# Two graph layers on one core: the plain fields of each step's edges are copied by ScalarE instead of GpSimd

## The chip, the cores and the metric

The kernel runs on one core of a Trainium2 chip. A core has five engines that run their own instruction streams and meet at semaphores: TensorE (PE in the profile, its weight loads PEld), VectorE (DVE), ScalarE (ACT), GpSimd (POOL) and SyncE (SP), which here only issues DMAs. The metric is the device time of one execution in microseconds (us); the median of three runs before the change is 1748.61 us (1748.29 to 1752.34).

## The reference

2500 nodes with 1024 features, 80000 edges sorted by destination, two layers:

```python
h = relu(layernorm(x));  x = x + segment_sum((h @ W0)[src] * edge_w[:, None], dst)
h = relu(layernorm(x));  # second layer: edges plus self loops, row = src, col = dst
hh = h @ W1.T + b;  deg = count(row);  norm = deg[row]**-0.5 * deg[col]**-0.5
x = x + segment_sum(norm[:, None] * hh[col], row)
```

## The kernel before

The sparse sums are done as dense products. The 2500 nodes are 20 tiles of 128 rows. For each tile of destinations the kernel builds the 128 x 2560 matrix of edge weights (stored as A, in two half-precision parts) and the matrix of edge counts (C), multiplies A by the support h @ W0 (first layer), and later C by the scaled h (second layer).

**How A and C are built.** A *window* is 4 destination rows; four windows are a *quad*, eight quads (q0 to q7) make a tile; there are 160 quads. A *step* takes 8 *touches*, blocks of 128 edges in a table `etab` in SBUF (four fields for each edge: a key, and the three "plain" fields: column, weight, rest of the weight). For a step of quad n:

- **fields** (GpSimd, L516 to L527): for each window a register load gives the block number (L522), a cast copies the three plain fields to `fbuf` (L525) and an addition writes the key (L527). Two slots of `fbuf`: the fields of a step wait until the one-hots of the step two before are done (`hots_ready`).
- **one_hots** (VectorE, L764 to L776): four operations (L769, L771, L774, L775) turn `fbuf` into the operands of the step's matmuls. They wait for the fields (`step_fields`) and for TensorE to have used the slot (`step_used`).
- **step** (TensorE, L1265): eight matmuls into a PSUM pair.
- **window_out** (ScalarE, L1048 to L1050): when the step is used, three copies from PSUM to a staging slot in SBUF; two staging slots, so it also waits for the DMA stores of the quad two before (`st_out`).
- **second_part** (VectorE, L820 and L823) and **sum_counts** (GpSimd, L540, the degrees) follow window_out; then SyncE stores the quad to DRAM (L346, L348).
- After a tile's last quad SyncE transposes the tile of A back from DRAM (L357), before it issues the stores of the next quads: its queue is in order.

The order is written out by hand. The quads 0 to 15 run among the support products. From quad 16 on a quad's step stands beside 15 matmuls of the dense product of an earlier tile (L1316), which is what fills TensorE. The quads 0 to 31 have 4 touches in a window, so two steps each; the other 128 have 2 touches and one step. VectorE's order in a quad n is one_hots(n), second_part(n - 1), then `further`, a register load and a branch (more edges, if a window has them); q1 has a residual in it as well (L838), q2 the moments (L848). GpSimd's order is fields of quad n + 1, then sum_counts(n - 1). The last 128 quads are in loops: VectorE and TensorE go round once for two tiles (16 quads), ScalarE once for one tile, GpSimd once for two quads. From 1090 us on the second layer runs, which the change doesn't touch.

Of the kernel before, what the change touches and what calls it, by code (L numbers as in the profile page):

```python
# [6 lines left out]
def gnn_two_layers(nc, x, src, dst, edge_weight, w0, w1, b1, out):  # L7
    f32, i32, f16 = mybir.dt.float32, mybir.dt.int32, mybir.dt.float16
    ALU = mybir.AluOpType
    ACT = mybir.ActivationFunctionType  # L10
    AX = mybir.AxisListType

    P = 128
    N, D = x.shape
    E = src.shape[0]
    T = -(-N // P)
    LAST = N - (T - 1) * P
    NCH = E // P
# [6 lines left out]
    QPT = WPT // 4  # L25
    NW = WPT * T
    NQ = NW // 4
    NB = NW // P
    UP, UL = 4, 2
    PRE = 2  # L30
    PQ = PRE * QPT
    UQ = 4 * QPT
# [7 lines left out]
    F = 4  # L40
# [20 lines left out]
    with ctx:  # L61
        def sb(name, shape, dt):
            return ctx.enter_context(nc.sbuf_tensor(name, shape, dt))

        def sem(name):
            return ctx.enter_context(nc.semaphore(name))
# [6 lines left out]
        fbuf = sb("fbuf", [P, FS + 1, F, 8, 2], f16)  # L73
# [7 lines left out]
        negbase = sb("negbase", [P, NW], f32)  # L81
# [73 lines left out]
        def hot(s):  # L155


            return slots[:, s * SS:(s + 1) * SS].rearrange("p (t c) -> p t c", c=CS)
# [3 lines left out]
        def twice(a, shape):  # L162

            return a.unsqueeze(len(shape) - 1).to_broadcast(shape)
# [5 lines left out]
        etab_c = etab[:, 0:CP * F].rearrange("p (c f) -> p c f", f=F)  # L170
# [18 lines left out]
        wtab = area[0:1, ROW:ROW + 4 * NW].bitcast(i32)  # L189
# [17 lines left out]
        etab_ready = sem("etab_ready")  # L207
# [15 lines left out]
        sup_hi = sem("sup_hi")  # L223
        sup_ready = sem("sup_ready")
        sup_free = sem("sup_free")
        step_fields = sem("step_fields")
        hots_plain = sem("hots_plain")
        hots_ready = sem("hots_ready")
# [53 lines left out]
        def win_pair(e, pre=False):  # L282

            return WIN if e == 0 or pre else TP

        def need(eng, s, value):

            if not isinstance(value, int) or value > 0:
                eng.wait_ge(s, value)
# [192 lines left out]
        def _(pool):  # L482
# [34 lines left out]
            def fields(n, s, v0, count, u):  # L517


                need(pool, hots_ready, n - 1)  # L520
                for w in range(count):
                    pool.load(regs, wtab[0:1, bass.ds((v0 + w) * 4, 1)])  # L522
                    c = pool.snap(regs[0], min_val=0, max_val=NCH)
                    at = slice(w * u, (w + 1) * u)
                    pool.tensor_copy(fbuf[:, s, 1:F, at].rearrange("p f u d -> p u f d"),  # L525
                                     twice(etab_c[:, bass.ds(c, u), 1:F], [P, u, F - 1, 2])).then_inc(step_fields, 1)
                    pool.tensor_tensor(fbuf[:, s, 0, at], twice(etab_c[:, bass.ds(c, u), 0], [P, u, 2]),  # L527
                                       twice(negbase[:, bass.ds(v0 + w, 1)], [P, u, 2]), ALU.add).then_inc(step_fields, 1)

            def step_pre(n):  # L530
                fields(n, n % 2, 2 * n, 2, UP)
# [12 lines left out]
            for t in range(STEP0, T):  # L544
# [10 lines left out]
                w = t - STEP0  # L555
# [21 lines left out]
        def _(dve):  # L577
# [178 lines left out]
            def columns(touches, n):  # L756
                return iota_r[:, 0:n].rearrange("p (n d) -> p n d", d=2).unsqueeze(1).to_broadcast([P, touches, n // 2, 2])

            def part(touches, a, n):
                return touches[:, :, a:a + n].rearrange("p t (n d) -> p t n d", d=2)  # L760
# [2 lines left out]

            def one_hots(n, s):  # L764

                dve.wait_ge(step_fields, 2 * UP_STEPS(n))

                need(dve, step_used, n - 1)
                nc.vector.tensor_tensor(part(hot(s), M0, SB), columns(8, SB), by_touch(s, 1, 8, SB),  # L769
                                        ALU.is_equal).then_inc(hots_plain, 1)  # L770
                nc.vector.tensor_tensor(part(hot(s), 0, P), columns(8, P), by_touch(s, 0, 8, P), ALU.is_equal)  # L771

                dve.wait_ge(hots_plain, n + 1)
                nc.vector.tensor_tensor(part(hot(s), W0C, SB), part(hot(s), M0, SB), by_touch(s, 2, 8, SB), ALU.mult)  # L774
                nc.vector.tensor_tensor(part(hot(s), W1C, SB), part(hot(s), M0, SB), by_touch(s, 3, 8, SB),  # L775
                                        ALU.mult).then_inc(hots_ready, 1)  # L776

            def UP_STEPS(n):

                return 2 * n + 2 if isinstance(n, int) and n < 2 * UQ else 4 * n - 4 * UQ + 4  # L780
# [246 lines left out]
        def _(act):  # L1027
# [9 lines left out]
            def window_out(n, s, steps_done, pre=False):  # L1037

                act.load(regs, wtab[0:1, bass.ds(n * 16 + 15, 1)])
                through = act.snap(regs[0], min_val=1, max_val=MOST + 1)  # L1040
                pair = win_pair(s, pre)
                sums = pair[:].rearrange("p (w x) -> p w x", w=4)

                need(act, st_out[s], STORED(n, s))
                need(act, win_sum, n - 1)
                act.wait_ge(step_used, steps_done)
                act.wait_ge(further_used, through)
                act.activation(c_stage(s), sums[:, :, 0:SB], ACT.Copy)  # L1048
                act.activation(a_stage(s)[:, 0], sums[:, :, SB:2 * SB], ACT.Copy, scale=A_DOWN)
                act.activation(a_stage(s)[:, 2], sums[:, :, 2 * SB:3 * SB], ACT.Copy, scale=A_DOWN).then_inc(win_act, 1)  # L1050

            def STORED(n, s):

                return 48 * (n // 2) if isinstance(n, int) else 24 * n - 24 * s

            def tile(td):
                for q in range(QPT):
                    n = QPT * (td + PRE) + q
                    window_out(n, q % 2, 2 * n + 2 if isinstance(n, int) and n < UQ else n + UQ + 1)

            def split_block(g):
# [8 lines left out]
            def std(g):  # L1070
                t0, n = X_GROUPS[g]
                act.wait_ge(var_ready, g + 1)
                act.activation(scale[:, t0:t0 + n], scale[:, t0:t0 + n], ACT.Sqrt).then_inc(std_ready, 1)
# [37 lines left out]
            for t in range(T):  # L1111
                if t > 0:
                    sup_first(t - 1)
                if t + 1 < T:
                    transposed(t + 1)
                if t + 2 < T:
                    rows_normal(t + 2)
                if t == 0:
                    std(2)
                if t == STEP0 - 1:  # L1120
                    act.wait_ge(table_ready, 1)
                if t == min(W1_AT):
                    act.wait_ge(w_pow, 2)
                for g in W1_AT.get(t, ()):
                    split_block(g)
                w = t - STEP0
                if 0 <= w < PQ:
                    if w in (1, 6, 9):
                        std({1: 3, 6: 4, 9: 5}[w])
                    window_out(w, w % 2, 2 * w + 2, True)  # L1130
            sup_first(T - 1)

            for td in range(UQ // QPT - PRE):
                tile(td)
            with act.Fori(UQ // QPT - PRE, T - PRE) as td:
                tile(td)

            def counts_first(e, done):
                act.wait_ge(self_ready[e], done)
# [330 lines left out]
```

## Time and profile before

| | |
|---|---|
| median of three runs | 1748.61 us |
| the profiled execution: its own time | 1750.08 us |
| its span, first to last instruction | 1748.3 us |
| granted TensorE clock, mean | 0.966 |
| busy: PE, DVE, ACT, POOL | 89%, 53%, 26%, 32% of the span |
| stretches: support and quads 0 to 15 / quads 16 to 31 / the loops | up to 392 / 398 to 513 / 513 to 1090 us |

A row of the timeline gives an instruction's start and duration in us, engine, line, operation, what it writes and reads, and in brackets the idle time of its engine before it with the one that released it. The engines with a q (POOLq, ACTq) are the sequencers that load registers and hand instructions to their engine.

### The profile page before, as it was taken

How to read it: one execution, taken by the hardware profiler on the slowest of the kernel's cores; microseconds unless marked ns; L12 is line 12 of the kernel's file. 1: busy time of each engine (PE TensorE's matmuls, PEld its weight loads, DVE VectorE, ACT ScalarE, POOL GpSimd, SP SyncE). 2: the span in 40 equal slices, each digit the busy share in tenths (PEclk: the TensorE clock that was granted, in tenths of full speed). 3: DMA queues.
4: the chain of work that ended last, by engine and by line, in shares of the span. 5: the costliest groups of instructions: out<-in, count | busy, mean ns of one | idle time of the engine just before them, and what ended most of it. 6: DMA issues, size and time to landing. Idle time of an engine off the chain costs nothing.

```text
span 1748.3 us, 30157 instructions
## 1 busy us (share of the span) xinstructions
PE 1554.0 (89%) x8627; PEld 792.7 (45%) x8628; DVE 930.2 (53%) x1747; ACT 456.5 (26%) x783; POOL 556.2 (32%) x1494
## 2 busy tenths in 40 slices
PE   2566699995979999999998999979999999999998
PEld 1233355543545454444554545334444444444443
DVE  6956556425977678777776776382313131313121
ACT  2514454531212222222222222271212121212110
POOL 0112444213656677677676774000000000000000
PEclk9977899997989999999999999999999999999999
DMA  7201242107546565666565666671232323232310
GB/s 262 97 1 32 64 139 61 29 16 165 114 97 141 125 142 135 144 145 139 133 151 129 146 140 150 201 230 55 63 99 66 96 66 96 66 96 66 96 37 25
DMA packets 449659, 185.86 MB, mean 106 GB/s; under 512 B 376677, under 2 KB 431993, under 8 KB 449544
## 3 DMA queue, kind: packets, MB, share of 16 engines
q1 hardware_dynamic: 449544, 184.63, 41.5%
q8 instruction: 34, 0.56, 0.1%
q14 instruction: 81, 0.66, 0.1%
HBM read 77.06 MB, written 77.11 MB: 88 GB/s over the span
## 4 chain that ended last, share of the span: by engine, by line
PE 54%; DVE 14%; issue 11%; POOLq 5%; POOL 5%; DMA 4%; SPq 4%; DVEq 2%; ACT 2%; ACTq 0%
PE pair L1392 19%; PE pair L1304 12%; PE pair L1253 9%; PE pair L1316 7%; PE pair L1265 5%; POOLq L522 3%; POOL fbuf L525 2%; SPq L357 2%; POOL fbuf L527 2%; DVE slots L774 2%; DMA a_scratch<-area 2%; DVE slots L775 2%; DVE h L939 1%; PE pair L1422 1%; SPq L378 1%
## 5 line engine op out<-in xcount | busy, mean ns | idle before, releaser
L1316 PE MATMUL pair<-h,area 128*128 128x512 f16 x2400 | 551.0, 383 | 2.6 <-issue 1.9
L1316 PEld LDWEIGHTS pair<-h,area 128*128 128x128 f16 x2400 | 234.2, 99 | 265.5 <-issue 18.2
L1265 PE MATMUL pair<-slots 128*128 128x240 f16 x1624 | 209.3, 275 | 104.8 <-DVE slots L775 54.6
L525 POOL CAST fbuf<-etab 128x12 f16 (+1 forms) x640 | 192.9, 301 | 152.4 <-DVE slots L775 79.2
L1048 ACT ACTIVATE area<-pair 128x320 f32<-128x320 f32 x160 | 69.9, 437 | 643.2 <-PE pair L1265 439.9
L1265 PEld LDWEIGHTS pair<-slots 128*128 128x128 f16 x1624 | 157.3, 100 | 171.4 <-issue 73.0
L979 DVE SCALAR_TENSOR_TENSOR agg_s<-pair,sc,agg_s 128x512 f16<-128x512 f32 x40 | 28.2, 747 | 350.7 <-ACT agg_s L1172 350.7
L1304 PE MATMUL pair<-wmat,agg_t 128*128 128x512 f16 x960 | 210.4, 379 | 1.6 <-ACT agg_t L1179 1.6
L527 POOL TENSOR_TENSOR fbuf<-etab,negbase 128x4 f16 (+2 forms) x640 | 200.9, 314 | 0.0
L1392 PE MATMUL pair<-h,etab 128*128 128x512 f16 x800 | 182.1, 379 | 8.9 <-DVE h L939 8.7
L1392 PE MATMUL pair<-h,slots 128*128 128x512 f16 x800 | 180.5, 379 | 0.0
L540 POOL TENSOR_TENSOR deg_acc<-deg_acc,area 128x320 f32<-128x320 f32 x160 | 144.0, 900 | 109.1 <-ACT area L1050 108.8
L769 DVE TENSOR_TENSOR slots<-iota_r,fbuf 128x640 f16<-128x640 f16 x192 | 99.3, 517 | 136.0 <-POOL fbuf L527 52.3
L1304 PEld LDWEIGHTS pair<-wmat,agg_t 128*128 128x128 f16 x960 | 92.3, 98 | 112.7 <-ACT agg_t L1179 1.8
L1253 PE MATMUL pair<-wmat,agg_t 128*128 128x512 f16 x480 | 114.7, 399 | 21.4 <-issue 21.4
L771 DVE TENSOR_TENSOR slots<-iota_r,fbuf 128x1024 f16<-128x1024 f16 x192 | 132.7, 691 | 0.0
L820 DVE SCALAR_TENSOR_TENSOR area<-pair,area 128x320 f16<-128x320 f32 x160 | 77.5, 484 | 93.4 <-ACT area L1050 93.2
L1253 PE MATMUL pair<-wmat,xt 128*128 128x512 f16 x480 | 108.8, 384 | 0.0
L1172 ACT ACTIVATE agg_s<-pair,sc 128x512 f16<-128x512 f32 x40 | 25.3, 683 | 314.1 <-PE pair L1394 314.1
L1392 PEld LDWEIGHTS pair<-h,etab 128*128 128x128 f16 x800 | 63.6, 97 | 82.0 <-DVE h L939 12.4
L774 DVE TENSOR_TENSOR slots<-slots,fbuf 128x640 f16<-128x640 f16 x192 | 98.6, 513 | 0.0
L775 DVE TENSOR_TENSOR slots<-slots,fbuf 128x640 f16<-128x640 f16 x192 | 98.5, 513 | 0.0
(181 smaller groups left out, 1316.1 us busy)
## 6 DMA issues: line engine op xcount, KB each, us to landing
c_scratch<-area SPq DMA_DIRECT2D x160, 160.0 KB, 2.2
a_scratch<-area SPq DMA_DIRECT2D x320, 80.0 KB, 2.2
area<-c_scratch SPq DMA_DIRECT2D x20, 1280.0 KB, 7.3
xt<-in_x SPq DMA_DIRECT2D x19, 512.0 KB, 3.6
x_scratch<-xt SPq DMA_DIRECT2D x19, 512.0 KB, 2.9
xt<-x_scratch SPq DMA_DIRECT2D x19, 512.0 KB, 3.6
out_x<-xt SPq DMA_DIRECT2D x19, 512.0 KB, 2.6
h<-x_scratch SPq DMA_DIRECT2D x4, 2048.0 KB, 10.5
```

Source lines behind the costliest of these rows:

```text
L525: pool.tensor_copy(fbuf[:, s, 1:F, at].rearrange("p f u d -> p u f d"), twice(etab_c[:, bass.ds(c, u), 1:F], [P, u, F - 1, 2])).then_inc(s ...
L527: pool.tensor_tensor(fbuf[:, s, 0, at], twice(etab_c[:, bass.ds(c, u), 0], [P, u, 2]), twice(negbase[:, bass.ds(v0 + w, 1)], [P, u, 2]), A ...
L540: pool.tensor_tensor(deg_acc[:], deg_acc[:], c_stage(s), ALU.add).then_inc(win_sum, 1)
L769: nc.vector.tensor_tensor(part(hot(s), M0, SB), columns(8, SB), by_touch(s, 1, 8, SB), ALU.is_equal).then_inc(hots_plain, 1)
L771: nc.vector.tensor_tensor(part(hot(s), 0, P), columns(8, P), by_touch(s, 0, 8, P), ALU.is_equal)
L774: nc.vector.tensor_tensor(part(hot(s), W0C, SB), part(hot(s), M0, SB), by_touch(s, 2, 8, SB), ALU.mult)
L775: nc.vector.tensor_tensor(part(hot(s), W1C, SB), part(hot(s), M0, SB), by_touch(s, 3, 8, SB), ALU.mult).then_inc(hots_ready, 1)
L1253: last = pe.matmul(dest[:, half * H:(half + 1) * H], h_t(t)[:, q, k, :], wmat[:, r, k, half * H:(half + 1) * H], start=k == q == r == 0, s ...
L1265: return pe.matmul(dest, touches[:, t, 0:P], touches[:, t, P:CS], start=first, stop=last, skip_group_check=True)
L1304: return pe.matmul(WO[:, half * H:(half + 1) * H], agg_t[:, q, k, :], wmat[:, r, k, half * H:(half + 1) * H], start=k == q == r == 0, stop ...
L1316: last = pe.matmul(sum_pair(e)[:, half * H:(half + 1) * H], wts(e)[:, q, k, :], hpart(k, r)[:, half * H:(half + 1) * H], start=k == q == r ...
L1392: pe.matmul(AGG[:, half * H:(half + 1) * H], lhs, h_of(q)[:, half * H:(half + 1) * H], start=first and q == 0, stop=last and q == 1, skip_ ...
```

## The change

ScalarE gets a function `fields` of its own, which loads the block number for each window and copies the three plain fields with an ACTIVATE; GpSimd keeps the key (L527) and the degrees (L540). There are two semaphores, `step_keys` and `step_fields`, and one_hots waits for both. ScalarE's copies for quad n + 2 stand directly ahead of window_out(n). ScalarE's loop is one iteration shorter, with the last tile written out behind it.

```diff
--- before.py
+++ after.py
@@ -223,6 +223,7 @@
         sup_hi = sem("sup_hi")
         sup_ready = sem("sup_ready")
         sup_free = sem("sup_free")
+        step_keys = sem("step_keys")
         step_fields = sem("step_fields")
         hots_plain = sem("hots_plain")
         hots_ready = sem("hots_ready")
@@ -522,10 +523,8 @@
                     pool.load(regs, wtab[0:1, bass.ds((v0 + w) * 4, 1)])
                     c = pool.snap(regs[0], min_val=0, max_val=NCH)
                     at = slice(w * u, (w + 1) * u)
-                    pool.tensor_copy(fbuf[:, s, 1:F, at].rearrange("p f u d -> p u f d"),
-                                     twice(etab_c[:, bass.ds(c, u), 1:F], [P, u, F - 1, 2])).then_inc(step_fields, 1)
                     pool.tensor_tensor(fbuf[:, s, 0, at], twice(etab_c[:, bass.ds(c, u), 0], [P, u, 2]),
-                                       twice(negbase[:, bass.ds(v0 + w, 1)], [P, u, 2]), ALU.add).then_inc(step_fields, 1)
+                                       twice(negbase[:, bass.ds(v0 + w, 1)], [P, u, 2]), ALU.add).then_inc(step_keys, 1)
 
             def step_pre(n):
                 fields(n, n % 2, 2 * n, 2, UP)
@@ -763,7 +762,8 @@
 
             def one_hots(n, s):
 
-                dve.wait_ge(step_fields, 2 * UP_STEPS(n))
+                dve.wait_ge(step_keys, UP_STEPS(n))
+                dve.wait_ge(step_fields, UP_STEPS(n))
 
                 need(dve, step_used, n - 1)
                 nc.vector.tensor_tensor(part(hot(s), M0, SB), columns(8, SB), by_touch(s, 1, 8, SB),
@@ -1049,6 +1049,26 @@
                 act.activation(a_stage(s)[:, 0], sums[:, :, SB:2 * SB], ACT.Copy, scale=A_DOWN)
                 act.activation(a_stage(s)[:, 2], sums[:, :, 2 * SB:3 * SB], ACT.Copy, scale=A_DOWN).then_inc(win_act, 1)
 
+            c_reg = [act.alloc_register("act_chunk")]
+
+            def fields(n, s, v0, count, u):
+
+
+                need(act, hots_ready, n - 1)
+                for w in range(count):
+                    act.load(c_reg, wtab[0:1, bass.ds((v0 + w) * 4, 1)])
+                    c = act.snap(c_reg[0], min_val=0, max_val=NCH)
+                    act.activation(fbuf[:, s, 1:F, w * u:(w + 1) * u].rearrange("p f u d -> p u f d"),
+                                   twice(etab_c[:, bass.ds(c, u), 1:F], [P, u, F - 1, 2]),
+                                   ACT.Copy).then_inc(step_fields, 1)
+
+            def fields_of(n, s):
+
+                if isinstance(n, int) and n < 2 * UQ:
+                    fields(n, s, 2 * n, 2, UP)
+                else:
+                    fields(n, s, 4 * n - 4 * UQ, 4, UL)
+
             def STORED(n, s):
 
                 return 48 * (n // 2) if isinstance(n, int) else 24 * n - 24 * s
@@ -1056,6 +1076,11 @@
             def tile(td):
                 for q in range(QPT):
                     n = QPT * (td + PRE) + q
+                    if isinstance(n, int) and n < UQ:
+                        fields_of(2 * n + 2, 0)
+                        fields_of(2 * n + 3, 1)
+                    elif not isinstance(n, int) or n + 2 < NQ:
+                        fields_of(n + UQ + 2, q % 2)
                     window_out(n, q % 2, 2 * n + 2 if isinstance(n, int) and n < UQ else n + UQ + 1)
 
             def split_block(g):
@@ -1119,6 +1144,9 @@
                     std(2)
                 if t == STEP0 - 1:
                     act.wait_ge(table_ready, 1)
+                    act.wait_ge(etab_ready, F)
+                    fields_of(0, 0)
+                    fields_of(1, 1)
                 if t == min(W1_AT):
                     act.wait_ge(w_pow, 2)
                 for g in W1_AT.get(t, ()):
@@ -1127,13 +1155,16 @@
                 if 0 <= w < PQ:
                     if w in (1, 6, 9):
                         std({1: 3, 6: 4, 9: 5}[w])
+                    fields_of(2 * w + 2, 0)
+                    fields_of(2 * w + 3, 1)
                     window_out(w, w % 2, 2 * w + 2, True)
             sup_first(T - 1)
 
             for td in range(UQ // QPT - PRE):
                 tile(td)
-            with act.Fori(UQ // QPT - PRE, T - PRE) as td:
+            with act.Fori(UQ // QPT - PRE, T - PRE - 1) as td:
                 tile(td)
+            tile(T - PRE - 1)
 
             def counts_first(e, done):
                 act.wait_ge(self_ready[e], done)
```

ScalarE in its loop, two windows' worth of the copies and the window_out behind them. Before (`area` is the window table on the register loads, the staging slot as an output of L1048 to L1050; pair is PSUM):

```order
L1039 ISA
L1039 TENSOR_LOAD area
L1040 ISA
L1046 REGISTER_ALU [waits win_sum,st_out1]
L1048 ACTIVATE area<-pair 128x320 [waits further_used,step_used]
L1049 ACTIVATE area<-pair 128x320
L1050 ACTIVATE area<-pair 128x320
```

And now, the last two of four windows ahead of window_out:

```order
L1059 ISA
L1059 TENSOR_LOAD area
L1060 ISA
L1061 ACTIVATE fbuf<-etab 128x2x3x2
L1059 ISA
L1059 TENSOR_LOAD area
L1060 ISA
L1061 ACTIVATE fbuf<-etab 128x2x3x2
L1039 ISA
L1039 TENSOR_LOAD area
L1040 ISA
L1048 ACTIVATE area<-pair 128x320 [waits further_used,step_used,win_sum]
```

Sixteen instructions (four windows) now stand between the wait for `hots_ready` and window_out's own register load. ScalarE's loop body goes from 60 such rows to 188.

GpSimd in its loop, one window. Before:

```order
L522 ISA
L522 TENSOR_LOAD area
L523 ISA
L525 COPY fbuf<-etab 128x2x3x2
L527 ISA
L527 TENSOR_TENSOR fbuf<-etab,negbase 128x4
```

Now:

```order
L523 ISA
L523 TENSOR_LOAD area
L524 ISA
L526 TENSOR_TENSOR fbuf<-etab,negbase 128x4
```

The register loads stay on GpSimd, and are there a second time on ScalarE.

VectorE's first operation of the one-hots in the loop, before and now:

```order
L769 TENSOR_TENSOR slots<-iota_r,fbuf 128x8x80 [waits step_used,step_fields]
```

```order
L769 TENSOR_TENSOR slots<-iota_r,fbuf 128x8x80 [waits step_used,step_fields,step_keys]
```

It has a third wait; nothing else moves on VectorE.

## Rows read from the trace of the kernel before

**Rows 1.** The page, the chain that ended last, by line.

```profile
PE pair L1392 19%; PE pair L1304 12%; PE pair L1253 9%; PE pair L1316 7%; PE pair L1265 5%; POOLq L522 3%; POOL fbuf L525 2%; SPq L357 2%; POOL fbuf L527 2%; DVE slots L774 2%; DMA a_scratch<-area 2%; DVE slots L775 2%; DVE h L939 1%; PE pair L1422 1%; SPq L378 1%
```

**Rows 2.** Groups, 513 to 1090 us: line, form xcount | busy us, mean ns | idle before.

```profile
L527 POOL TENSOR_TENSOR fbuf<-etab,negbase 128x4 f16 x496 | 163.2, 329 | 0.0
L525 POOL CAST fbuf<-etab 128x12 f16 x496 | 148.9, 300 | 88.9 <-issue 55.7 <-DVE slots L775 23.7
L1265 PE MATMUL pair<-slots 128*128 128x240 f16 x1012 | 127.5, 270 | 42.2 <-DVE slots L775 35.3 <-DVE slots L812 6.3
...
L1048 ACT ACTIVATE area<-pair 128x320 f32<-128x320 f32 x127 | 55.5, 437 | 438.6 <-PE pair L1265 277.5 <-DMA a_scratch<-area 161.2
```

**Rows 3.** Timeline of VectorE and GpSimd at a one_hots.

```profile
924.61 0.20 POOL L527 TENSOR_TENSOR fbuf<-etab,negbase 128x4 f16 x1
926.36 0.49 DVE L769 TENSOR_TENSOR slots<-iota_r,fbuf 128x640 f16<-128x640 f16 x1 [0.56 <-POOL fbuf L527]
```

**Rows 4.** Sequencers, by source line: duration min/median/max in ns.

```profile
L522 POOLq TENSOR_LOAD <-area x640: 283/291/823, 87.2 to 1072.9; - x160
...
L527 POOLq FUSED_REGOPS  x640: 37/52/58, 87.9 to 1073.4; - x160
...
L1039 ACTq TENSOR_LOAD <-area x160: 272/279/644, 107.4 to 1076.4; - x160
```

**Rows 5.** Timeline of GpSimd, two windows in the loop, and the first behind a one_hots.

```profile
914.58 0.19 POOL L525 CAST fbuf<-etab 128x12 f16 x1
...
915.26 0.19 POOL L525 CAST fbuf<-etab 128x12 f16 x1 [0.33 <-issue]
...
943.08 0.19 POOL L525 CAST fbuf<-etab 128x12 f16 x1 [3.23 <-DVE slots L775]
```

**Rows 6.** Timeline, 923.9 to 942.6 us: VectorE, ScalarE, TensorE from q4 to the next q0.

```profile
923.94 0.48 DVE L775 TENSOR_TENSOR slots<-slots,fbuf 128x640 f16<-128x640 f16 x1
925.67 0.44 ACT L1048 ACTIVATE area<-pair 128x320 f32<-128x320 f32 x1 [2.98 <-DMA a_scratch<-area]
927.77 0.48 DVE L775 TENSOR_TENSOR slots<-slots,fbuf 128x640 f16<-128x640 f16 x1
928.18 0.48 DVE L820 SCALAR_TENSOR_TENSOR area<-pair,area 128x320 f16<-128x320 f32 x1
928.69 0.90 DVE L823 TENSOR_TENSOR area<-area 128x320 f16<-128x320 f16 x1
929.59 0.49 DVE L769 TENSOR_TENSOR slots<-iota_r,fbuf 128x640 f16<-128x640 f16 x1
929.61 0.44 ACT L1048 ACTIVATE area<-pair 128x320 f32<-128x320 f32 x1 [2.84 <-PE pair L1265]
931.01 0.48 DVE L775 TENSOR_TENSOR slots<-slots,fbuf 128x640 f16<-128x640 f16 x1
931.41 0.48 DVE L820 SCALAR_TENSOR_TENSOR area<-pair,area 128x320 f16<-128x320 f32 x1
934.95 0.48 DVE L820 SCALAR_TENSOR_TENSOR area<-pair,area 128x320 f16<-128x320 f32 x1
940.56 0.49 DVE L769 TENSOR_TENSOR slots<-iota_r,fbuf 128x640 f16<-128x640 f16 x1 [4.19 <-issue]
942.52 0.99 PE L1265 MATMUL pair<-slots 128*128 128x240 f16 x8 [1.59 <-DVE slots L775]
```

**Rows 7.** Timeline: SyncE's transposes, VectorE from q4 to q7 of the next tile.

```profile
947.57 5.74 SPq L357 DMA_TRANSPOSE area<-a_scratch  x2
...
961.30 0.48 DVE L775 TENSOR_TENSOR slots<-slots,fbuf 128x640 f16<-128x640 f16 x1
...
976.20 0.49 DVE L820 SCALAR_TENSOR_TENSOR area<-pair,area 128x320 f16<-128x320 f32 x1 [0.32 <-ACT area L1050]
```

**Rows 8.** Timeline of TensorE: a step in quads 16 to 31, and a long wait.

```profile
492.00 0.99 PE L1265 MATMUL pair<-slots 128*128 128x240 f16 x8 [0.75 <-DVE slots L775]
...
603.58 1.78 PE L1265 MATMUL pair<-slots 128*128 128x240 f16 x8 [3.30 <-DVE slots L775]
```

## The prediction

> **What bounds the kernel now.** I read the page first, then the groups of the loop stretch, then the timeline of one turn of the loop. The chain gives the second layer's matmuls the largest share, where the change does nothing, and then three small shares to GpSimd: 3% to its register loads and 2% each to cast and key [rows 1]. Read by itself that says: 7% of 1748 us, some 120 us, hang on GpSimd. The groups say how little TensorE loses by it: from 513 to 1090 us it waits 42.2 us for VectorE ahead of its steps, 35.3 of them for the last one-hot operation [rows 2]. And the timeline says that even these are not GpSimd's: the one-hots at 926.36 are put down to the key of L527, but the last key of their step ended at 924.81, 1.55 us earlier [rows 3] (the four windows of a step end before the sum_counts that follows them, so the key at 924.61 is this step's last). In the loop I paired each one-hot operation with its fields in this way, and none began within 0.3 us of the last key. What holds VectorE there is its own register load and branch between second_part and one_hots.
>
> So what makes TensorE wait in the loop? Three places in each turn of 16 quads, some 71 us. At A and C (q4 of either tile) the transposes hold SyncE for 5.74 us [rows 7], the stores wait behind them, ScalarE waits for the staging slot (161.2 us in the stretch [rows 2]) and VectorE for ScalarE. At B (q0 of the odd tile) VectorE stands 4.19 us with nothing to wait for but its own instructions, at its loop's end [rows 6]. TensorE then waits 1.59 us, since VectorE was not 4 us ahead. Behind A and C VectorE starts with no lead and has three quads to regain one, and how much it has when the next place comes is what decides.
>
> **The change part by part.**
>
> *GpSimd loses 496 casts in the loop and 640 in all, 300 ns each* [rows 2]. It is worth nothing by the pairing above: no one-hots wait for it. Nor does it free VectorE much: the long second operation of second_part, 0.90 us at 928.69, ends at 929.59, just when the next one-hots start [rows 6], and these could hardly have started earlier, since the register load and branch run beside it; what lengthens it is the degree sum, which stays. I take 0. The bounds: nothing below, and above, half of what TensorE waits for one-hots, 35.3 / 2 = 18 us gained.
>
> The Trainium skill (SBUF — State Buffer, Who interferes with whom) says that GpSimd and VectorE take a shared port pair as an exclusive lock for a whole instruction, and ScalarE never waits on anyone there. By that rule alone each cast moved away could free VectorE for up to its own time, some 0.2 us, 128 quads by four by 0.2 being 100 us at most; the rows decide against it, as VectorE's lengthened operations stand beside the degree sum.
>
> *ScalarE gains 640 register loads and copies.* Its idle time in the stretch, 438.6 us [rows 2], holds them easily as a sum. What matters is their place: between the end of one_hots(n), for which they wait, and window_out(n). What four windows cost there is not in the trace for ScalarE; the nearest rows are GpSimd's. From the end of a one-hot step to the first cast: 943.08 less 942.46, 0.62 us [rows 5, 6] (L775 at 941.98 took 0.48). From one window to the next 0.68 us (915.26 less 914.58) [rows 5], of which the key's own register operation, 52 ns and its hand-over, is some 0.12 [rows 4], so 0.56. Then window_out's own load and waits, some 0.7: the load is 279 ns on ScalarE, 291 on GpSimd [rows 4], with as many small operations behind it. Sum: 0.62 + 3 x 0.56 + 0.7 = 3.0 us from one_hots(n) to window_out(n). It needs 1.1 (three copies), so VectorE can start second_part(n) at 4.1 us. Bounds for the 3.0: 1.4, what it is now (929.61 less 928.25 [rows 6]), if the loads run ahead of the waits, and 3.4 with 0.68 a window. Where VectorE leads TensorE by over 2 us, this is no later than now (a step takes 0.98 and then ScalarE starts). Where it has no lead, ScalarE is up to 2 us late.
>
> *The walk from A to B* [rows 6]. One_hots(q4) ends at 924.42 either way. Window_out(q4) begins at 925.67 now, and then at 924.42 + 3.0 = 927.4; its copies end at 928.5, and second_part(q4), at 928.18 now, starts 0.3 later. One_hots(q5) ended at 928.25: window_out(q5) goes from 929.61 to 931.3, ends at 932.4, and second_part(q5), 931.41 now, starts 1.0 later. One_hots(q6) ended at 931.49, then at 931.9: second_part(q6) can start at 936.0, against 934.95, 1.1 later. From there only VectorE's 4 us at the loop's end and the one-hots follow, on which TensorE waits already: 1.1 us at each B, and second_part(q7) behind it, whose store starts the transposes that time C, moves along. Seven such places: 7.7 us.
>
> *From C to A* [rows 7]. One_hots(q4) ends at 961.78. The same steps give second_part(q4) 0.8 later, q5 0.9, q6 1.5, q7 1.2 (976.20 to 977.4), and its store, the next transposes and A are as late. Two of the seven C places are followed by steps at the lower clock, where TensorE itself gives VectorE 1.7 us or more; I count five by 1.2: 6.0 us.
>
> *VectorE's third wait.* An instruction more on its sequencer ahead of one_hots. From 398 to 513 us, with two steps in a quad, TensorE waits in nearly every quad for VectorE, 0.75 us at 492.00 [rows 8], and VectorE is never idle for another reason. I take 0.07 for 16 quads, 1.1 us; between 0 and 0.3 us each. In the loop it is inside the rounding of the walk.
>
> *Before 398 us and after 1090 us: 0.* TensorE is busy with support products there and ScalarE's copies stand in front of a window_out that waits for a step anyway; the second layer is not touched. Up to 2 us either way.
>
> Sum: 7.7 + 6.0 + 1.1 = 14.8 us on the profiled execution's 1750.08, so 1764.9; that execution lies 1.5 above the median of the runs (1748.61), so 1763.4 as a median; I say 1763.
>
> **The rivals.**
>
> *Hidden.* ScalarE's copies are ready earlier than I count: if its sequencer loads ahead, 1.4 us in place of 3.0, window_out is where it was and only the third wait is left. 1748 to 1752, say 1750. For it: ScalarE's idle time. Against: the load of each window stands behind the wait for hots_ready, and GpSimd's rows show how such a run goes.
>
> *Faster.* The chain is right: one-hots in catch-up wait for GpSimd, and two engines halve that. The place is the quads behind A and C and the quads 16 to 31; the price is a quarter of the 0.56 us by which VectorE idles before an operation put down to L527 [rows 3], 0.14 us, in some 55 quads behind these places and 16 more: 10 us, so 1740. It decides if fields end within 0.1 us of the one-hots, which the pairing excludes in the loop.
>
> *Dearer: ScalarE's loop end.* VectorE's body of some 1000 instructions costs it about 4 us at a turn (4.19 [rows 6]). ScalarE's goes from 60 to 188 and turns at each tile. If it pays as much, 3 to 4 us, the end of even tiles is hidden by VectorE's own stand, but that of odd ones makes window_out(q0) and (q1) 3 late: part of it meets the wait at A, and if 1.5 to 2 us of each of seven come through, 14 us more: 1777. The Trainium skill (Runtime: NRT & Kernel Launch, Instruction fetch mechanics) says that a branch taken to a target outside two pages of 256 instructions has to fetch the page; by that VectorE's cost agrees with the trace, and ScalarE's body would pay wherever a page boundary falls inside it.
>
> *Dearer: the clock.* After the wait of 3.30 us at 603.58 the eight matmuls took 1.78 us and not 0.99 [rows 8]. With each wait 1 us longer more of them can be like that; it is part of the same case, up to 10 us.
>
> **How the numbers follow.** Forecast 0.56, hidden 0.17, faster 0.10, dearer 0.17. 0.3% is 5.2 us, about what a measurement can tell from no change: the forecast and the dearer cases are slower, 0.73; hidden is the same, 0.17; faster 0.10. The forecast's own range is 1756 to 1772 (walk by 0.6 to 1.5 us a place). For 8 in 10 it goes down to 1748, into the hidden case, and up to 1780.
>
> **What would show it.** On ScalarE four L1061 some 0.56 us apart, the first 0.6 behind L775, and window_out 3 us behind L775 at q4 to q6; VectorE's idle time before L820 put down to ScalarE grows from under 0.1 us to 0.5 or more at q5 to q7; TensorE's waits before L1265 grow from 35 to about 49 us; L540's company is unchanged. I am wrong if the copies come closer than 0.4 us apart, if L820 never waits behind A and C, or if the one-hots' starts move forward with GpSimd's shorter row of work. A stretch of over 2 us on ScalarE's sequencer at its loop's end speaks for the dearer case.

## The result, and the profile after

The changed kernel takes 1758.1 us in the median of 4 runs (1757.2 to 1761.7), against 1748.45 for the kernel before beside it; the ratio is 1.0054, 95% interval 1.0034 to 1.0074, so 9.4 us slower, between 5.9 and 12.9. The forecast was 1763, with 1748 to 1780 as its range. The profiled execution took 1758.42 us with a span of 1756.6, where the sum of the prediction said 1764.9.

The page after, the chain that ended last, by engine:

```profile
PE 49%; DVE 15%; issue 8%; SPq 8%; DMA 7%; ACTq 6%; ACT 4%; DVEq 2%; POOLq 0%; POOL 0%
```

GpSimd's three shares of [rows 1] are gone, and the kernel is slower all the same: ScalarE's sequencer has them now. A chain names what was passed through, not what an edit there would give.

The groups after, 513 to 1090 us, in the order of [rows 2] and then the new line and VectorE's two operations of second_part:

```profile
L526 POOL TENSOR_TENSOR fbuf<-etab,negbase 128x4 f16 x496 | 163.9, 332 | 146.6 <-issue 106.3 <-DVE slots L775 33.4 <-ACT area L1050 3.9
L1296 PE MATMUL pair<-slots 128*128 128x240 f16 x1008 | 124.7, 267 | 42.6 <-DVE slots L775 41.5
L1048 ACT ACTIVATE area<-pair 128x320 f32<-128x320 f32 x126 | 55.1, 437 | 116.5 <-DMA a_scratch<-area 49.9 <-issue 44.8 <-PE pair L1296 21.5
L1061 ACT ACTIVATE fbuf<-etab 128x12 f16 x496 | 106.0, 215 | 223.6 <-issue 123.0 <-DVE slots L775 99.7
L820 DVE SCALAR_TENSOR_TENSOR area<-pair,area 128x320 f16<-128x320 f32 x126 | 61.3, 487 | 78.2 <-ACT area L1050 78.1
L823 DVE TENSOR_TENSOR area<-area 128x320 f16<-128x320 f16 x126 | 66.7, 530 | 4.3
```

The casts moved as said, and TensorE's waits for L775 grew from 35.3 to 41.5 us, not to 49. L823 went down by 12 us; the prediction had called its company, the degree sum, unchanged. The two of them before, and the sum after:

```profile
L823 DVE TENSOR_TENSOR area<-area 128x320 f16<-128x320 f16 x127 | 78.9, 621 | 4.4
L540 POOL TENSOR_TENSOR deg_acc<-deg_acc,area 128x320 f32<-128x320 f32 x127 | 112.2, 884 | 95.4 <-ACT area L1050 95.3
```

```profile
L539 POOL TENSOR_TENSOR deg_acc<-deg_acc,area 128x320 f32<-128x320 f32 x126 | 113.2, 899 | 162.0 <-ACT area L1050 161.9
```

The sum itself is as long as it was, but GpSimd now stands ready for it, 162 us in place of 95: it begins within 0.2 us of the end of ScalarE's copies 55 times of 127 before and 100 of 125 after (78 of 127 in "no casts" below). An L823 that runs beside no sum takes 325 ns, one beside the sum 677 before and 571 after in the mean: it meets a shorter part of it.

The timeline after behind A, the stretch of [rows 6], 4.4 us later:

```profile
928.34 0.48 DVE L775 TENSOR_TENSOR slots<-slots,fbuf 128x640 f16<-128x640 f16 x1
...
929.76 0.21 ACT L1061 ACTIVATE fbuf<-etab 128x12 f16 x1 [1.48 <-DVE slots L775]
930.58 0.21 ACT L1061 ACTIVATE fbuf<-etab 128x12 f16 x1 [0.61 <-issue]
...
931.11 0.21 ACT L1061 ACTIVATE fbuf<-etab 128x12 f16 x1 [0.32 <-issue]
931.68 0.21 ACT L1061 ACTIVATE fbuf<-etab 128x12 f16 x1 [0.35 <-issue]
...
932.32 0.44 ACT L1048 ACTIVATE area<-pair 128x320 f32<-128x320 f32 x1 [0.43 <-issue]
...
933.45 0.49 DVE L820 SCALAR_TENSOR_TENSOR area<-pair,area 128x320 f16<-128x320 f32 x1 [0.76 <-ACT area L1050]
```

L775 ends at 928.82, the first copy comes at 929.76 (elsewhere 0.63 us behind), and window_out 3.5 us behind the one-hots, where it was 1.25 in [rows 6]. VectorE is ready for L820 at 932.69 and stands 0.76 us for ScalarE.

TensorE's first step of quad 64 and of quad 158, before and then after:

```profile
657.43 0.99 PE L1265 MATMUL pair<-slots 128*128 128x240 f16 x8 [0.79 <-DVE slots L775]
...
1075.26 0.98 PE L1265 MATMUL pair<-slots 128*128 128x240 f16 x8
```

```profile
654.29 0.99 PE L1296 MATMUL pair<-slots 128*128 128x240 f16 x8 [2.03 <-DVE slots L775]
...
1084.30 0.99 PE L1296 MATMUL pair<-slots 128*128 128x240 f16 x8 [0.26 <-DVE slots L775]
```

These 94 quads take 417.8 us before and 430.0 after: 12.2 us, all of the loss and more. The changed kernel is ahead by 3.1 us when they begin; that need not be the change's doing, since the kernel "third wait" below, where GpSimd keeps its casts and ScalarE copies no fields, is ahead of the profiled execution of before by 4.7 us there.

An undisturbed quad takes 4.06 us from step to step. What each quad of a turn takes beyond that, mean of the turns between these two rows (worked out from the starts of TensorE's steps; six turns, at B with the one whose wait ends at the first row; the other rows are the experiments below; C is q4 of the tile that begins with B, and the columns with a prime are the other tile, with A at its q4; the last column is the time of the 94 quads):

```
                  B q0   q1    q2+q3  C q4   q5    q6+q7  q2+q3'  A q4'  q5'   94 quads
before            1.11   0.25  0.42   2.46   0.32  0      0       1.60   0.04  417.8
changed           2.42   1.06  0.62   1.40   0.04  0.31   1.32    1.15   0.04  430.0
spare copies      2.75   1.23  0.19   1.32   0.04  0.17   0.74    2.00   0.31  432.4
half of these     1.12   0.26  0.33   2.61   0.32  0      0       1.37   0.04  416.5
third wait        1.12   0.23  0      2.82   1.42  0      0       1.09   0.04  420.5
no casts          1.13   0.23  0.73   1.99   0.32  0      0       1.20   0.19  415.0
copies behind     1.28   0.23  0.78   1.94   0.32  0      0       1.34   0.11  416.5
one load          1.59   0.51  0.27   1.93   0.32  0      0       1.30   0.04  415.8
GpSimd one load   1.04   0.23  0.55   2.47   1.39  0      0       1.30   0.04  422.4
no sums           0.99   0.23  0      2.81   1.11  0      0       1.05   0.47  420.4
no sums, casts    0.73   0.23  0      2.82   1.68  0      0       0.83   0.39  420.6
```

The table says where the change costs: 1.3 us at B, 0.8 in the quad behind it, 1.3 in q2 and q3 of the tile in which A lies, while C and A themselves get shorter by 1.1 and 0.5. That they do so because TensorE has waited already is likely, but no run separates it.

Each row is one profiled execution. Before and "third wait" differ by 2.7 us in the last column, while the medians of their runs lie 1.6 us apart with 0 inside the interval; so a few us between two rows say little by themselves. A good part of such differences are quads of some 1.65 us more at a mean granted clock of 0.70 to 0.75. Among the quads behind B, C and A, the kernel before has one of these, the changed kernel three, spare copies five (one of them the quad behind the last A), third wait five, and half of the copies one.

### The profile page after: what moved, and what is told of

It is laid out like the page before. It is cut to its first block, busy times and chain, and to the rows that moved or that the text cites. A ratio compares the mean times of both kernels' runs of the same rounds, so it can differ in the third digit from the quotient of the medians.

```text
span 1756.6 us, 31275 instructions
## 1 busy us (share of the span) xinstructions
PE 1561.5 (89%) x8627; PEld 789.9 (45%) x8628; DVE 919.9 (52%) x1747; ACT 585.5 (33%) x1423; POOL 409.2 (23%) x854
## 4 chain that ended last, share of the span: by engine, by line
PE 49%; DVE 15%; issue 8%; SPq 8%; DMA 7%; ACTq 6%; ACT 4%; DVEq 2%; POOLq 0%; POOL 0%
PE pair L1423 19%; PE pair L1335 12%; PE pair L1284 10%; SPq L358 5%; DMA a_scratch<-area 5%; ACTq L1059 4%; PE pair L1296 3%; PE pair L1347 3%; DVE slots L774 2%; DVE slots L775 2%; DVE area L820 1%; DVE slots L771 1%; DVE h L939 1%; ACT fbuf L1061 1%; DVE slots L769 1%
## 5 line engine op out<-in xcount | busy, mean ns | idle before, releaser
L526 POOL TENSOR_TENSOR fbuf<-etab,negbase 128x4 f16 (+2 forms) x640 | 205.1, 326 | 228.2 <-issue 110.9
L1061 ACT ACTIVATE fbuf<-etab 128x12 f16 (+1 forms) x640 | 136.8, 216 | 278.2 <-issue 141.1
L1048 ACT ACTIVATE area<-pair 128x320 f32<-128x320 f32 x160 | 69.9, 437 | 246.3 <-PE pair L1296 116.0
L820 DVE SCALAR_TENSOR_TENSOR area<-pair,area 128x320 f16<-128x320 f32 x160 | 77.8, 486 | 98.6 <-ACT area L1050 98.5
L1423 PEld LDWEIGHTS pair<-h,etab 128*128 128x128 f16 x800 | 63.7, 97 | 80.8 <-DVE h L939 10.8
L775 DVE TENSOR_TENSOR slots<-slots,fbuf 128x640 f16<-128x640 f16 x192 | 96.6, 503 | 0.0
```

The costliest lines, as they stand in the source:

```text
L1061: act.activation(fbuf[:, s, 1:F, w * u:(w + 1) * u].rearrange("p f u d -> p u f d"), twice(etab_c[:, bass.ds(c, u), 1:F], [P, u, F - 1, 2] ...
L1423: pe.matmul(AGG[:, half * H:(half + 1) * H], lhs, h_of(q)[:, half * H:(half + 1) * H], start=first and q == 0, stop=last and q == 1, skip_ ...
```

## Experiments

Each was timed in five rounds beside the kernel before, on the same chip. That kernel's median was 1748.2, 1748.9 and 1752.4 us for the three groups of four, so what is compared are the ratios, turned into us with 1748.6.

**Spare copies.** The cost of ScalarE's place alone, without GpSimd's relief and without the third wait.

```diff
+ act.activation(spare[:, s, 1:F, w * u:(w + 1) * u]..., twice(etab_c[:, bass.ds(c, u), 1:F], ...), ACT.Copy).then_inc(spare_in, 1)
```

> The kernel before, where GpSimd still makes all fields, and ScalarE in addition makes the changed kernel's 640 loads and copies at their place, into a tile that nobody reads (it waits, beside the one-hots, for its own copies of two steps ago). The theory (the place ahead of window_out is the whole cost, GpSimd's lost casts are worth nothing): the time of the changed kernel, 1758 us, within 3. The rival (GpSimd's relief gives something back, which hid part of the cost): slower than the changed kernel by what the relief gives, 1762 to 1770 us.

Measured 1762.1 us, ratio 1.0076 [1.0062, 1.0090]: 13.3 us. The place is dearer than the whole change, so the rival in this expectation is right: something gives back. The third wait (below) added, some 5 us are given back in the changed kernel (1.0054 against 1.0076 and 1.0009); the three intervals together leave nearly 5 us to either side of that.

**No casts.** The relief alone.

```diff
- pool.tensor_copy(fbuf[:, s, 1:F, at]..., ...).then_inc(step_fields, 1)
```

> GpSimd without its plain casts and nobody in its place: the plain fields of steps 0 and 1 stay for all steps (this is what the kernel leaves out), keys and degrees as in the kernel before. It has no third wait. The theory: the casts are on no path, 1748 us, within 2 of before. The rival (relief): under 1744 us, in the best case 1738, with one-hots that start earlier behind the places A and C.

Measured 1737.9 us, ratio 0.9951 [0.9936, 0.9967]: 8.6 us faster. My value of 0 is wrong. L823 now (same columns and stretch as above):

```profile
L824 DVE TENSOR_TENSOR area<-area 128x320 f16<-128x320 f16 x127 | 64.4, 507 | 4.4
```

**Third wait.**

```diff
- dve.wait_ge(step_fields, 2 * UP_STEPS(n))
+ dve.wait_ge(step_keys, UP_STEPS(n))
+ dve.wait_ge(step_fields, UP_STEPS(n))
```

> The kernel before with two semaphores for its fields, so that VectorE waits for keys and plain fields apart; GpSimd does both as before. The theory: 0.07 us in each of 16 quads, 1749.5 us, in all between 1748 and 1752. The rival (VectorE's instruction more is also paid in the loop, in each catch-up): above 1753 us.

Measured 1749.0 us, ratio 1.0009 [0.9997, 1.0021], 1.6 us with 0 inside the interval: nothing that speaks against the 1.1 of the sum, and nothing that shows it.

**Copies behind.** Four slots, the copies for the step four ahead.

```diff
- fields_of(n + UQ + 2, q % 2)
- window_out(n, q % 2, ...)
+ window_out(n, q % 2, ...)
+ fields_of(n + UQ + 4, q % 4)
```

> The changed kernel with four slots for the plain fields, so that ScalarE's copies for the step four ahead stand behind window_out(n) and not ahead of it; as many loads and copies, the same third wait. The theory (the place is the cost): the loss goes, 1745 to 1750 us; VectorE's waits ahead of L820 behind A and C are again under 0.1 us. The rival (the copies cost wherever they stand, by ScalarE's longer row of work or its access to the tables): 1755 us or more. A copy that runs when window_out(n+1) could start may cost up to 1 us a place, so 1750 to 1754 would be the theory with part of the price left.

Measured 1740.4 us, ratio 0.9951 [0.9933, 0.9970]. As many copies, as much work on each engine, and 18 us faster than the changed kernel. VectorE's waits for ScalarE:

```profile
L820 DVE SCALAR_TENSOR_TENSOR area<-pair,area 128x320 f16<-128x320 f32 x127 | 61.3, 483 | 62.9 <-ACT area L1050 62.9
```

The loss is a matter of place, and nothing of it is left: the time is that of the kernel without casts. It beats both kernels. (The two slots more came with the new place and were not tried alone; spare copies and half of them, with two slots, test the place by itself.)

**Half of the spare copies.** The dose: two windows in place of four ahead of window_out.

```diff
- fields(n, s, 4 * n - 4 * UQ, 4, UL)
+ fields(n, s, 4 * n - 4 * UQ, 2, UL)
```

> The kernel with spare copies on ScalarE (1762 us), in the loop with two windows in place of four, so that window_out(n) comes some 2.0 us behind one_hots(n) and not 3.1. If the loss is a matter of lateness that has a cover (up to about 2.4 us nothing is lost, as the kernel with one load says), it goes nearly whole: 1747 to 1752 us. The rival (each copy ahead of window_out costs its share, in proportion): half of the 13 us stay, 1754 to 1757 us.

Measured 1749.1 us, ratio 0.9982 [0.9967, 0.9996]. Not half of the 13.3 us stays, but none (it is even 3.1 us below before, which nothing here explains), and its row of the table is near that of before at every place. Window_out comes 1.9 us behind the one-hots at B in the median of the turns, 3.3 us with all four windows, and 1.1 in the kernel before. Lateness has a cover; where it ends, beyond 1.9 and before 3.3 us, this run doesn't say.

**One load.** The same copies at the same place, with one register load.

```diff
- act.load(c_reg, wtab[0:1, bass.ds((v0 + w) * 4, 1)])
+ act.load(c_reg[0:count], wtab.rearrange("o (v a) -> o v a", a=4)[0:1, bass.ds(v0, count), 0])
```

> The changed kernel, where ScalarE loads the four chunk numbers of a step with one register load in place of four; the copies stay ahead of window_out. The theory (the loss is the time from one_hots to window_out): that falls from some 3.1 us to under 2.2, and of the 17 us between this place and the version with copies behind window_out (1740 us) about half go: 1747 to 1752 us. The rival (a load takes as long by its numbers, or the loss hangs on the copies themselves): 1756 us or more.

Measured 1742.4 us, ratio 0.9962 [0.9949, 0.9975], 16 us faster than the changed kernel and better than expected. ScalarE's sequencer (min/median/max in ns), and q5 behind A in the timeline, where L775 ends at 923.50:

```profile
L1058 ACTq TENSOR_LOAD <-area x192: 468/889/1776, 86.9 to 1065.1; - x192
```

```profile
924.73 0.58 ACT L1061 ACTIVATE fbuf<-etab 128x12 f16 x4 [0.97 <-issue]
925.75 0.44 ACT L1048 ACTIVATE area<-pair 128x320 f32<-128x320 f32 x1 [0.44 <-issue]
```

The load of four numbers takes some 890 ns, not much under four of 277, but the four copies then take 0.58 us together, and window_out comes 2.25 us behind the one-hots in place of 3.0 (at B 2.35 in place of 3.25). Those 0.75 to 0.9 us are worth about 16: with them all of the place's 13 us go, within the noise.

**No sums**, and **no sums, no casts**. How the casts cost, tested by taking away the degree sum.

```diff
- pool.tensor_tensor(deg_acc[:], deg_acc[:], c_stage(s), ALU.add)
+ pool.tensor_tensor(deg_acc[:, :, 0:1], deg_acc[:, :, 0:1], c_stage(s)[:, :, 0:1], ALU.add)
```

> The kernel before, GpSimd still making all fields, where the degree sum adds one column of each window in place of all 80 (the other degrees are left out). The theory, formed from the run without casts (8.6 us faster; L823 64.4 us busy from 513 to 1090 us and not 78.9): what GpSimd's casts cost is that the degree sum starts 0.3 us later and lies on VectorE's L823 in the catch-up. Then a kernel without the long sum must gain at least as much: 1730 to 1741 us, and L823 takes 0.33 us in the mean. The rival (the one-hots wait for the fields in the catch-up, which this kernel makes no earlier): 1745 to 1748 us.

> As the kernel without sums, and also without GpSimd's plain casts (the fields of steps 0 and 1 stay). The theory (casts cost by way of the sum alone): as fast as without sums, within 3 us. The rival (fields that are late): 6 to 9 us faster than without sums.

Measured 0.9948 [0.9932, 0.9964] and 0.9950 [0.9934, 0.9965]: 9.1 and 8.7 us faster, the same. Without the long sum the casts cost nothing, as the theory says. But the place is not the one it named. L823 of the first of them, then its L775 at quads 16 and 32, and the same two of the kernel before:

```profile
L823 DVE TENSOR_TENSOR area<-area 128x320 f16<-128x320 f16 x126 | 41.3, 327 | 4.3
```

```profile
394.42 0.48 DVE L775 TENSOR_TENSOR slots<-slots,fbuf 128x640 f16<-128x640 f16 x1
...
492.03 0.48 DVE L775 TENSOR_TENSOR slots<-slots,fbuf 128x640 f16<-128x640 f16 x1
```

```profile
397.08 0.48 DVE L775 TENSOR_TENSOR slots<-slots,fbuf 128x640 f16<-128x640 f16 x1
...
500.51 0.48 DVE L775 TENSOR_TENSOR slots<-slots,fbuf 128x640 f16<-128x640 f16 x1
```

97.6 us for these 16 quads in place of 103.4: 5.8 us, 0.36 in each quad. In this stretch TensorE waits for VectorE in most quads of the kernel before (0.4 to 0.75 us in nine of them), and in the kernel without sums in one, beside a wait of 14 us that both have; so a shorter L823 is felt there at once. In the 94 quads the kernel without sums gains nothing (420.4 us), although L823 is at its shortest: what it wins at A and B goes at C and in the quad behind (table), of which four in six run at the lower clock, and in before one. That led to the next.

**GpSimd one load.** The kernel before with a shorter row of GpSimd's work.

```diff
- pool.load(regs, wtab[0:1, bass.ds((v0 + w) * 4, 1)])
+ pool.load(regs[0:count], wtab.rearrange("o (v a) -> o v a", a=4)[0:1, bass.ds(v0, count), 0])
```

> The kernel before (GpSimd makes all fields) with one register load of the four chunk numbers on GpSimd in place of four; nothing on ScalarE. If casts cost by way of a late degree sum alone, then a shorter row of GpSimd's work gains by the same way: its windows come closer by 0.15 us each, 1742 to 1747 us. The rival (the sum's start does not hang on the loads, because the ScalarE copies before it end later): 1748 us, no change.

Measured 1750.9 us, ratio 0.9986 [0.9971, 1.0002]: 2.4 us faster with 0 inside, so neither theory is told apart. L823 and TensorE at C (then its granted clock, PEclk, in three stretches):

```profile
L823 DVE TENSOR_TENSOR area<-area 128x320 f16<-128x320 f16 x127 | 66.1, 520 | 4.4
```

```profile
962.41 1.62 PE L1265 MATMUL pair<-slots 128*128 128x240 f16 x8 [2.26 <-DVE slots L775]
963.82 4.49 PE L1316 MATMUL pair<-h,area 128*128 128x512 f16 x15
```

```profile
957.00:962.00 5.00, 3.15 (x15) 1.24 (x13) 2.60 (x6) 2.19 (x6) 2.26 (x5) 1.00 0.50 109
962.40:966.80 4.40, 4.39 (x17) 2.31 (x18) 3.40 (x8) 1.09 (x3) 3.87 (x15) 0.61 0.78 212
967.00:971.00 4.00, 4.00 (x25) 2.24 (x23) 2.76 (x6) 1.09 (x3) 3.48 (x10) 1.00 0.39 82
```

L823 is nearly as short as without casts (520 ns, 507 there), and the 94 quads take 422.4 us and not 415.0. The first of TensorE's two rows is its step at C. In the three stretches below them the figure behind the five engines' busy times is the granted clock: it is 0.61 from 962.40 to 966.80, so most of this quad runs at the lower level, 1.2 GHz. It takes 5.75 us in place of 4.10, and this happens at five of six C; at one of six in the kernel without casts. 4 x 1.65 = 6.6 of the 7.4 us between them.

**Both one load**, **copies behind with one load**, **keys ahead**. Three that might have been better still; the first two join edits shown above, and the third is copies behind with this:

```diff
- step_loop(i * 2 + s + 1, 1 - s)
- sum_counts(i * 2 + s - 1, 1 - s)
+ sum_counts(i * 4 + s - 1, (s - 1) % 2)
+ step_loop(i * 4 + s + 4, s)
```

> The changed kernel with one load of four numbers on ScalarE (1742 us) and on GpSimd as well. If GpSimd's row still delays the degree sum in the catch-up, 2 to 4 us faster: 1738 to 1741 us. If what the sum costs there is gone already: 1742 us.

> Four slots, copies behind window_out (1740 us), with one load of four numbers on both engines. ScalarE's copies are ahead by four steps there, so their length is of no use; only GpSimd's can be: 1737 to 1740 us. The rival (a shorter row of copies lets the next window_out start earlier at A and C): under 1737 us.

> The kernel with ScalarE's copies behind window_out, and GpSimd's keys in four slots as well: GpSimd makes the keys of the step four ahead, and the degree sum stands in front of them. By the theory the sum starts as soon as ScalarE's copies end, and no one-hots wait for a key: 1733 to 1740 us. The rival: a sum that starts with second_part lies on L823 each time, and what was won is lost: 1742 to 1748 us.

Measured 0.9962 [0.9945, 0.9979], 0.9955 [0.9938, 0.9972] and 1.0012 [1.0000, 1.0024]. The first two are the same as without GpSimd's part (0.9962, 0.9951): a shorter row of GpSimd's work gives nothing more. The third loses what copies behind had won, 11 us: its quads 16 to 32 take 2.4 us more than there, the 94 quads 424.3 us against 416.5. A sum that starts first is no help. It does not cost by the way that the rival in its expectation names: L823 takes 499 ns there, less than the 509 of copies behind. Four quads behind C or A at the lower clock against one are about 5 us of the 7.8; what makes the rest was not tried.

## Why the prediction was right, and where it was not

*ScalarE's place, 13.7 us in the sum: right as a sum, in part by luck.* The spare copies say 13.3 [10.8, 15.7]. Copies came 0.53 us apart (0.56 said), window_out 3.0 to 3.5 us behind the one-hots (3.0 said). At B the table has 1.3 us a place, where the walk gave 1.1. So the first half of the walk, with its cost and its wait, is what happened. The second half is not.

*From C to A: wrong in its way, and not 1.2 us a turn.* The walk carried 1.2 us through the last store and the transposes to A. A became shorter, and so did C. A loss does lie ahead of A, at q2 and q3, 1.3 us a turn; but from C to A taken together (table, C q4 to q5') the changed kernel wins 0.2 us a turn and spare copies loses 0.2. What stands in the measured sum in the place of these 1.2 us is the quad behind B, told next, which the sum didn't have. That the two are alike in size is luck. After, VectorE at q1 and q2 of A's tile and TensorE's step:

```profile
914.15 0.49 DVE L820 SCALAR_TENSOR_TENSOR area<-pair,area 128x320 f16<-128x320 f32 x1 [1.15 <-ACT area L1050]
...
917.48 1.14 DVE L774 TENSOR_TENSOR slots<-slots,fbuf 128x640 f16<-128x640 f16 x1
918.54 0.48 DVE L775 TENSOR_TENSOR slots<-slots,fbuf 128x640 f16<-128x640 f16 x1
...
919.08 0.99 PE L1296 MATMUL pair<-slots 128*128 128x240 f16 x8 [0.71 <-DVE slots L775]
```

The late window_out makes VectorE wait 1.15 us at q1, the residual and the moments follow, and VectorE has no lead left. I had walked only the quads behind a wait, and took for granted that VectorE leads elsewhere.

*The quad behind B, 0.8 us a turn (1.0 with spare copies): not in the sum.* It is the clock, which the prediction named as a part of the dearer case with up to 10 us: in three of six turns the quad behind B takes 5.9 us and not 4.3. After, the quad ahead of B's step and the one behind it, from 947.37, behind a wait of 2.05 us; the granted clock is 1.00 and then 0.71:

```profile
941.10:947.30 6.20, 4.22 (x24) 2.14 (x22) 2.71 (x7) 1.92 (x7) 2.36 (x6) 1.00 0.55 140
947.40:953.30 5.90, 5.85 (x23) 2.58 (x24) 4.12 (x9) 2.68 (x11) 2.34 (x7) 0.71 0.28 57
```

In before no quad behind B did (4.28 to 4.33); it had one slow quad behind C among the six, and the changed kernel none.

*GpSimd's lost casts, 0: this is the step that failed.* Alone they are worth 8.6 us [5.8, 11.2]. Beside ScalarE's copies they are worth about 5, which is only what is left between 13.3 for the place, 1.6 for the third wait and the 9.4 measured; it is no check of its own. It is also the difference between the 9.4 us measured and the 14.8 of the sum. The pairing of one-hots with fields was sound, since without the long sum the casts cost nothing. It answered the wrong question. I wrote that the degree sum "stays" as VectorE's company; it stays, but it starts when GpSimd's row lets it. With the casts away L823 loses 14 us of its 79, and 15 between spare copies (82.1) and the changed kernel (66.7). How much of the 8.6 us comes by this way is not settled: of the 9.8 us between the spans of the profiled executions the 94 quads hold 2.9, quads 16 to 32 1.4 and quads 32 to 64 2.3, and in the last two stretches third wait and half of the copies, which keep all casts, are shorter by 1.1 to 1.2 and 1.7 to 2.0 as well. Nor does L823's length decide the time: GpSimd's one load has it nearly as short as without casts, and third wait has it at 85.5 us, longer than before, and both take as long as before within their intervals. What is shown is that casts and long sum cost together: without the sum, taking the casts away gives nothing more.

*The sentences on the shared port:* by the rule of the Trainium skill (SBUF — State Buffer, Who interferes with whom), a lock for a whole instruction, the casts themselves would have held VectorE up. The runs agree with it for the long sum and show nothing of it for the casts: L823 takes 621 ns before and 327 without the long sum, but with the sum gone it takes 327 ns with casts and 325 without. The casts count by when the sum comes. The bound of 100 us is far off, and my 0 as well.

*The third wait, 1.1:* 1.6 [-0.5, 3.7] measured, not to be told from 0. (VectorE is not quite "never idle for another reason" in quads 16 to 32: L820 at 429.86 waits 14.88 us for ScalarE in the kernel before, and as long in the changed one.)

*The rivals.* Hidden: refuted, the loads do not run ahead. Faster by GpSimd's chain: there is a gain, as large as the 10 us written there, but by another way, and more than paid for. Dearer by ScalarE's loop end: refuted. The branch's row alone doesn't say so, since VectorE's has much the same length (after, min/median/max in ns):

```profile
L1165 ACTq COMPARE_BRANCH  x15: 40/45/54, 540.7 to 1055.0; - x15
```

```profile
L880 DVEq FUSED_REGOPS  x8: 98/98/98, 495.6 to 1018.8; - x8
...
L880 DVEq COMPARE_BRANCH  x8: 50/56/56, 576.0 to 1089.8; - x8
```

It is the row behind the branch that tells. VectorE turns back at 1015.57 and its next row begins at 1018.79; over its seven turns the gap is 2.75 to 3.17 us. On ScalarE it is 0.14 to 0.16 us, all 15 times.

By the rule of the Trainium skill (Runtime: NRT & Kernel Launch, Instruction fetch mechanics) this body would have paid where a page's boundary fell inside it; 188 instructions paid nothing that a row shows. Whether a boundary falls inside them no run shows.

## What to carry to other kernels

Work that moves to an idle engine is paid by what it stands in front of there: ask which handover is queued behind it, and by how much that may be late. Here 2.3 us cost nothing that was measured and 3.0 to 3.5 cost 13 us, and two slots more with the copies behind window_out, or one register load in place of four, turned a loss of 9 us into a gain of 7 to 9. And an operation that is on no path can still set when the next one on its engine starts, and what that one will lie on.

## What the runs showed of the hardware

ScalarE's 192 register loads of "one load" took 889 ns in the median; the first 64 of them load two numbers and the rest four, strided, at some 890 ns, and a load of a single number took 277 ns. Behind a load of four ScalarE's small copies (214 ns each) began 0.12 us apart. The Trainium skill (Runtime: NRT & Kernel Launch, Instruction fetch mechanics) puts a register load at some 200 ns a register, a figure it gives beside loads from HBM; these, from the window table, agree with it at four (some 222 ns each), and one by itself cost more.

A wait of TensorE at C is not worth its length. In the 14 kernels profiled, six C each, the quad with the wait took 6.6 us or more 27 times; the next quad then took 5.4 to 5.8 us, at a lower granted clock, 21 times. Where it took less than 6.6 us, 9 of 57. (6.6 is taken here because it parts the cases well; no run tests it.) So a few tenths more of waiting at one place can cost 1.65 us behind it, and the same waiting spread over q2 to q4, as without casts or with copies behind (0.7 to 0.8 us in q2 and q3, 1.9 to 2.0 at C), has one slow quad in six and not five. What exactly decides is open: in the kernel before quads of 6.54 and 7.25 us were followed by fast ones, and one of 6.39 by a slow one.
